# Layer 0 of a two-layer attention and MoE kernel: operand parts stored in three transfers over all 128 partitions, with the two halves inside the term in DRAM

## The reference

```python
xn = _layernorm(x)
qkv = jnp.einsum('btd,ed->bte', xn, w_in) + b_in          # 16 heads of 8
scores = jnp.einsum('bhqd,bhkd->bhqk', q, k) * scale
scores = jnp.where(jnp.abs(diff) <= 128, scores, -1e30)
ctx = jnp.einsum('bhqk,bhkd->bhqd', jax.nn.softmax(scores), v)
x1 = x + xn + ctx @ w_out.T + b_out + ffn_int8(xn)
```

## Time and profile before

| | |
|---|---|
| Median of 3 runs | 729.73 us (728.58 to 729.93) |
| The profiled execution | 732.44 us |
| Its span, first to last instruction | 730.4 us |
| Layer 0's main loop in that span | about 60 to 425 us |
| PE, DVE, ACT, POOL busy | 79%, 64%, 47%, 43% |
| Mean granted clock of PE | 0.942 |

### The profile page before, as it was taken

How to read it: one execution, slowest core, us unless ns; L and a number is a source line. 1 busy time by engine, 2 the same in 40 slices (tenths; PEclk the granted TensorE clock), 3 DMA queues, 4 the chain that set the end, 5 groups by cost and what they waited for, 6 DMA issues and landing times. The chain is left out here.

```text
span 730.4 us, 18096 instructions
## 1 busy us (share of the span) xinstructions
PE 575.6 (79%) x5741; PEld 360.6 (49%) x5742; DVE 465.4 (64%) x1896; ACT 341.5 (47%) x1037; POOL 316.1 (43%) x361
## 2 busy tenths in 40 slices
PE   2378887888888978889799849988972699999930
PEld 0135554555554545555465426666542366666620
DVE  3688767686777776766777037888875254445425
ACT  2202563654645646447466635655641244444410
POOL 6950533443332435423100014788874155555530
PEclk9999999999999999999999989999987699999975
DMA  2845036171381542702600223111211122222209
GB/s 58 176 99 103 31 81 125 31 162 46 74 160 32 119 87 59 169 25 69 136 18 18 75 77 149 57 58 45 71 54 49 34 74 76 73 76 73 76 15 345
DMA packets 51140, 61.18 MB, mean 84 GB/s; under 512 B 9841, under 2 KB 41973, under 8 KB 49280
## 3 DMA queue, kind: packets, MB, share of 16 engines
q1 hardware_dynamic: 45568, 49.73, 29.2%
q0 software_dynamic: 4352, 8.47, 3.5%
q10 hardware_dynamic: 1152, 2.10, 0.7%
HBM read 32.08 MB, written 28.45 MB: 83 GB/s over the span
## 5 line engine op out<-in xcount | busy, mean ns | idle before, releaser
L571 DVE CUSTOM_DVE_ANT_0 A<-A,band 128x320 f32<-128x320 f32 (+2 forms) x512 | 213.7, 467 | 92.6 <-PE A L729 91.7
L464 ACT ACTIVATE Pb<-SB 128x320 f32<-128x320 f32 (+2 forms) x512 | 176.2, 403 | 162.2 <-PE SB L759 159.0
L729 PE MATMUL A<-Ks,Qs 48*64 48x320 bf16 (+2 forms) x1024 | 151.3, 303 | 10.9 <-DVE mneg L571 9.7
L750 PE MATMUL SB<-Qs,Ks 50*64 50x320 bf16 (+2 forms) x1024 | 145.9, 290 | 3.6 <-ACT Pb L464 2.9
L759 PE MATMUL SB<-ends,ident 64*64 64x64 bf16 (+1 forms) x1024 | 106.7, 206 | 0.0
L1518 POOL DMA_INDIRECT results<-y,xt x72 | 70.7, 982 | 71.5 <-issue 37.6
L750 PEld LDWEIGHTS SB<-Qs,Ks 50*64 50x64 bf16 x1024 | 57.0, 107 | 58.5 <-issue 29.5
L729 PEld LDWEIGHTS A<-Ks,Qs 48*64 48x64 bf16 x1024 | 57.6, 110 | 48.5 <-DVE mneg L571 36.1
L1622 PE MATMUL UP<-w_up,xT 128*128 x144 | 80.1, 639 | 1.7 <-ACT xT L1531 1.2
L770 PE MATMUL PV<-Pb,Va 128*32 128x320 f32 (+2 forms) x1024 | 77.2, 422 | 0.0
L1080 POOL DMA_INDIRECT expert_rows<-pay,pos x64 | 62.9, 983 | 24.0 <-issue 17.8
(11 more groups left out here) (194 smaller groups left out, 973.4 us busy)
## 6 DMA issues: line engine op xcount, KB each, us to landing
Qs<-parts_dram SPq DMA_DIRECT2D x16, 384.0 KB, 6.1
Ks<-parts_dram SPq DMA_DIRECT2D x16, 384.0 KB, 8.9
xt<-expert_rows SPq DMA_DIRECT2D x72, 65.0 KB, 1.8
yb<-results SPq DMA_DIRECT2D x8, 512.0 KB, 6.8
parts_dram<-qp SPq DMA_DIRECT2D x16, 192.0 KB, 2.8
parts_dram<-kp SPq DMA_DIRECT2D x16, 192.0 KB, 2.8
l_xb<-x_dram SPq DMA_DIRECT2D x9, 256.0 KB, 3.0
xb<-in_x SPq DMA_DIRECT2D x8, 256.0 KB, 3.0
```

The lines of the kernel that those rows point to most:

```text
L464: act.activation(Pb[:, group % 4, c, 0:w], SB[k % NB_BANKS][:, 0:w], ACT.Exp).then_inc(act_exp, 1)
L571: nc.vector.tensor_tensor_reduce(scores_of, scores_of, band[:, skip:skip + w], -1.0, 3e38, ALU.add, ALU.min, mneg[:, step % 2, col:col + 1 ...
L729: mm = nc.tensor.matmul(A[k % NA_BANKS][r0:r0 + HP, 0:w], Qs[b % RING][rows, a, HP * sub:HP * sub + HP], Ks[b % RING][rows, a, lo:lo + w], ...
L750: nc.tensor.matmul(out[r0:r0 + HP, 0:w], Ks[b % RING][rows, a, HP * sub:HP * sub + HP], Qs[b % RING][rows, a, lo:lo + w], start=True, stop ...
```

## The change

In `parts_dram` the parity moves inside the term: [batch, q or k, parity, term, 64, 512] becomes [batch, q or k, term, parity, 64, 512]. Both parities of a part are then one run of 128 rows in each term, and a store takes all 128 partitions of the tile: three DMAs (384, 256 and 128 KB) in place of six. The load still takes one parity per DMA. The six terms of one parity are no longer one contiguous block: from one term to the next there are 128 rows of 512 in place of 64, and the source is written with the term as an axis of its own. The count that the waits ask for follows.

```diff
-    parts_dram = nc.dram_tensor("parts_dram", [NB, 2, 2, NTERM, HP, T], BF16).ap()
+    parts_dram = nc.dram_tensor("parts_dram", [NB, 2, NTERM, 2, HP, T], BF16).ap()
...
-    PARTS = 16 * 2 * len(QRUNS)
+    PARTS = 16 * len(QRUNS)
...
-            for par in range(2):
-                for n, count, part, width in runs:
-                    src = tile[HP * par:HP * par + HP, part:part + width, :]
-                    if width < count:
-                        src = src.to_broadcast([HP, count, T])
-                    sp.dma_start(parts_dram[g, which, par, n:n + count].rearrange("n r t -> r n t"), src)\
-                        .then_inc(done, 16)
+            for n, count, part, width in runs:
+                src = tile[:, part:part + width, :]
+                if width < count:
+                    src = src.to_broadcast([P, count, T])
+                sp.dma_start(parts_dram[g, which, n:n + count].rearrange("n q r t -> (q r) n t"), src)\
+                    .then_inc(done, 16)
...
                     sp.dma_start(tile[pg][r0:r0 + MROW].rearrange("r a t -> r (a t)"),
-                                 parts_dram[g, which, par].rearrange("n (d a) t -> (n d) (a t)", a=NA))\
+                                 parts_dram[g, which, :, par].rearrange("n (d a) t -> n d (a t)", a=NA))\
                         .then_inc(dma_stack, 16)
```

## The result

| | before | changed |
|---|---|---|
| Median | 729.83 us (728.58 to 732.56, 4 runs) | 754.41 us (749.29 to 756.25, 4 runs) |
| Ratio, 95% interval | 1 | 1.032 (1.0259 to 1.0382) |
| Profiled execution, its span | 732.44, 730.4 us | 749.29, 747.2 us |
| Mean granted clock of PE | 0.942 | 0.925 |

The ratio on record, 1.032, is not the quotient of the two medians, which is 1.034 (24.6 us). The profiled execution of the changed kernel is its fastest of four, 5.1 us under its median, and that of the kernel before is 2.6 us above its own: so the two profiles differ by 16.8 us, and 7.7 of the 24.6 us stand in no profile.

What follows compares the result with a forecast made beforehand. The prediction found PE waiting only for DVE or ACT in layer 0, no DMA setting the pace. Slower loads would add 2.6 + 4.7 + 0.5 + 32 - 4 = +36 us to the median 729.73: 766 us, range 731 to 786.

Steps and rivals of the forecast that it cites:

- No DMA bounds layer 0, and the loads' slack is 2 to 6 us: Layer 0: PE waits 49.6 us, none for a DMA; load slack 5.7 us in batch 1, 1.7 in batch 2.
- The stores gain nothing by themselves: K and Q stores: three issues take 1.8 us in place of 3.9; 728 at best if loads keep 16 engines.
- An outer axis of 6 gives six engines: Loads of Qs and Ks: source 6 x 8 x 4096 in place of 48 x 4096 gets six engines, not 16.
- The row at 0.13: Earlier trace, place_max of line 210: DMA share 0.13 of 16, two engines, its outer dimension; evidence for six engines.
- 19.7 us of data for a load: Four load DMAs per batch: 256 KB per engine at 13.3 GB/s, 4.9 us a DMA, 19.7 us together.
- D: Rival on load pace: 15 to 18 GB/s per engine, 14.6 to 17.5 us, total 731 to 750 us; chance 0.18.
- 80 GB/s or less: Sign in the load stages: DMA share near 0.38 at 80 GB/s or less would show the forecast right.
- A: Rival: six engines at their own 26.7 GB/s, loads 9.8 us, 730 us total; above 18.2 not slower; chance 0.07.
- Lateness: PE's first use of loads: late 2.6 us in batch 0, 4.7 in batch 1, 32 over batches 2 to 7.
- The clock at nothing, up to 10 us in the bound: PE clock falling to 1.2 GHz after waits: charged nothing, up to 1.5 us a batch, 10 in the upper bound.
- 4 us given back, by PE's waits for mneg: PE's waits for mneg, 7.0 us: half, about 4 us, given back as DVE and ACT catch up.
- 0.5 us for the stores of base behind the load: Batch 1: base stores queued behind the load delay GpSimd's norm; 0.5 us charged, up to 3 above.

Runs made afterwards that it cites:

- e5_rows_early: Changed kernel with q and k rows reordered so loads have one stride, and K stores ahead of place_max; 766.01 us against 766.21 for the kernel before, ratio 0.9998.
- e1_rows: Changed kernel with q and k rows reordered by permuting the weights, so a load's 48 rows have one stride; 729.03 us, ratio 0.9993 to the kernel before.
- e4_four: Changed kernel loading only the first four of six terms, last 16 rows of Qs zero; 735.57 us, one run.
- e2_pad: Kernel before, six stores kept, with 8 rows of padding behind each term in DRAM; 768.58 us, ratio 1.0539 to the kernel before.
- e3_early: Changed kernel with the K stores issued ahead of place_max; 736.75 us, ratio 1.0114 to the kernel before.
- e7_warm: e2_pad with 32 more matmuls, results overwritten, ahead of each wait for loads; 807.91 us on a second chip, ratio 1.0507 to the kernel before.
- e6: e3_early with batch 0's base store ahead of batch 1's loads; 771.37 us on a second chip, ratio 1.0065 to the kernel before.
- e9: e6's kernel word for word on a third chip; 769.97 us, ratio 1.0069 to the kernel before.

## Why the prediction was right, point by point

1. **No DMA bounds layer 0, and the loads' slack is 2 to 6 us**: right. e5_rows_early, the earliest loads of all, is at 0.9998. The size of the slack is a reading of the earlier trace rows that no run tests by itself.
2. **The stores gain nothing by themselves**: right; e1_rows, 0.9993. Their sizes: three issues took 1.58 us against my 1.8, and the data ran at 344 GB/s, so my 2.3 us for 768 KB holds (2.3 at 344). In batch 2 the three issues took 2.69 us, not 1.8; there the loads began with less of a lead.
3. **An outer axis of 6 gives six engines**: shown by the share of 0.34, by 0.25 for an axis of 4 (e4_four), by 16 engines when the axis is 48 again (e1_rows), and by the padding alone (e2_pad). The row at 0.13 was enough to forecast it. The Trainium skill's rule ("DMA: Bandwidth & Descriptors", section "Why a DMA increments its semaphore by 16 and not by 1") agrees with all four.
4. **19.7 us of data for a load**: the term that was mis-sized. Issue to landing for batch 2 was 18.2 us where I had 21.9; less the same 2.2 of fixed part that is 16.0 us, or 256 KB at 16.4 GB/s on the slowest engine, between my 13.3 and the deciding 18.2. It is the case that I had listed as D (14.6 to 17.5 us). But one term does not fit all batches: from first issue to first use it was 17.8, 18.2, 18.3 and 17.4 us in batches 1, 2, 5 and 6, at most 17.3 in batches 3 and 4, which did not wait, and 21.1 in batch 7, near my 21.9. In batch 7 the share fell to 0.13 from 373 to 377 us, two engines' worth still at work and 34 GB/s: the landing came some 4 us after most of them had done their part, and the pace in mid-load does not show it. Why that load was slower is open. Per busy engine it was 22.6 GB/s in mid-load, so if pairs hinder each other, it is not all the time. The port table of the Trainium skill ("SBUF - State Buffer", section "Door 1: The DMA port swizzle") says which rows meet; the four-term load, which has no such pair by it, ran at 25.8. How two engines share in time neither page nor run shows. Of the signs that I had named, the share came (0.34 against 0.38) and the 80 GB/s or less did not: 123 GB/s lies midway between it and the 160 of A.
5. **Lateness**: 2.6 + 4.7 + 32 us of waits forecast, 10.7 measured, with 5.30 for batch 7 and 1.97 for batch 2. With 16.0 in place of 19.7 the working of the prediction gives 128.5 - 3.7 - 123.16 = 1.6 us for a batch, 10 for six, nothing for batch 0 and 1.0 for batch 1 (3.7 less than 2.6 and 4.7); the trace has no wait for a load before 60 us and one of 0.67 in batch 1. The mechanism was right, and this one number carried most of the error. That the sum comes out at 10 is in part luck: the same wait once a batch, as forecast, did not come. Two batches waited for nothing and batch 7 made half of the sum; of batch 2's 1.97 us, 1.1 are its stores' longer issue (point 2).
6. **The clock at nothing, up to 10 us in the bound**: too low. Layer 0 ended 16.5 us later with 10.7 us of waits. The other 5.8 stand beside 27 us more at 1.2 GHz (51 against 24, in windows of 1 us); in e2_pad it is 6.4 beside 51 us more, in e3_early 0.3 beside 3. That is 0.21, 0.13 and 0.1 us for each us at the lower level. The added time stands mostly where PE waited for loads. Of two neighbouring windows of the changed kernel, the first has no such wait and the clock of the kernel before (0.96), the second has the wait of batch 5:

```profile
204.00:252.00 48.00, 40.57 (x568) 25.35 (x564) 34.36 (x157) 26.35 (x76) 18.86 (x21) 0.96 0.29 90
252.00:300.00 48.00, 40.66 (x533) 25.07 (x527) 33.01 (x152) 25.72 (x74) 17.22 (x20) 0.89 0.29 89
```

   So a part of the loss is likely the clock's; but e7_warm, made to isolate it, did not, and the share is argued, not shown. Nor do single profiles hold a few us: e1_rows, which waits for no load and has the kernel before's time, ended layer 0 at 420.7, 3.3 us before it.
7. **4 us given back, by PE's waits for mneg**: wrong place. Those stayed (7.0, then 7.2); PE's waits for ctxn, 10.2 us before, fell to 7.7. The 2.5 are in the right direction and smaller. The line of the kernel before:

```profile
PE misc L736 <- DVE ctxn L592: 10.2, 7, 1.5
```

8. **0.5 us for the stores of base behind the load**: POOL's wait grew from 21.2 to 27.5 us and DVE then waited 0.6 us for it. Its full price may be larger: by this edit alone pass B of batch 1 began 4.1 us earlier than in e3_early in one profile (e6) and 2.9 in the other (e9, 108.41 us), and layer 0 ended 3.3 and 0.4 us earlier. With such a spread the price stays open.

The range of 731 to 786 held. The median, 754, even lies at the lower end of the forecast's own range, 752 to 782, but in part by luck: the waits were D's, and with 16.0 us the prediction's sum would have been some 737. Two things lie between that and 754. Layer 0 lost 5.8 us beyond its waits, where I had put the clock at nothing and 4 us as given back. And the medians differ by 7.7 us more than the two profiles do. Those 7.7 us have no profile; e9_base_again makes waits that differ from run to run likely.

## What to carry to other kernels

When a layout changes to make one side of a DRAM round trip simpler, write out the access pattern of the other side: an outer axis of 6 in place of 48 leaves 6 of 16 DMA engines, and a share of 0.34, missing times to landing and a longer issue are what tells of it. Choose the layout so that both sides have one outer axis that 16 divides; here a permutation of the rows did it for nothing (ratio 0.9993). And price a slower transfer by its slack first: the same loads on six engines cost 3.2% with the K stores behind place_max and 1.1% with them ahead of it.

## What was not expected of the hardware

- Six engines on 48 partitions moved 123 GB/s in mid-load where sixteen moved 157 to 175: most of the speed with 3/8 of the engines. An engine's pace on the same target fell from 22.6 to about 10 GB/s as ten more joined. Over a whole load it is less: 16.0 us of data (batch 2) against 9.2 (batch 1 of the kernel before).
- The issue of a load took SP 0.68 to 0.77 us on six engines (median) and 0.42 on sixteen; a store of 384 KB over 128 partitions landed in 2.6 us, no later than one of 192 KB over 64 did (2.8), and a store took 0.49 us to issue in place of 0.61 (medians over all sizes).
- After PE had waited for a load for 1.18 to 5.30 us, the clock was granted at 1.2 GHz for 7 to 10 us at a stretch (0.50 from 126.9 to 133.7 us behind the wait of 1.97 us), and 32 more matmuls ahead of the wait did not prevent it (e7_warm). With the wait of 5.30 us, 371.9 to 377.2, it fell while PE still stood:

```profile
372.70:382.90 10.20, 4.88 (x39) 2.31 (x41) 2.20 (x10) 1.03 (x3) 0.00 (x0) 0.50 0.07 20
```
